# Attention on one core: the turned outputs and maxima leave the scores' banks for the maxima's banks, and VectorE reads them

## What is computed

```python
scores = jnp.einsum('bhqd,bhkd->bhqk', q, k) / jnp.sqrt(jnp.float32(HEAD_DIM))
causal = jnp.tril(jnp.ones((t, t), dtype=bool))          # first layer only
scores = jnp.where(causal[None, None], scores, -jnp.inf)
attn = jax.nn.softmax(scores, axis=-1)
out = jnp.einsum('bhqk,bhkd->bhqd', attn, v)
```

## Time and profile before

| what | us |
| --- | --- |
| median of 3 runs | 5106.11 |
| lowest, highest | 5089.62, 5106.27 |
| the profiled execution | 5106.96 |
| its span, first to last instruction | 5105.2 |
| its mean granted TensorE clock | 0.967 of full |

### The profile page before, as it was taken

The page is one execution under the profiler, slowest core; times in us unless marked ns, Lnnn a source line. Parts: engine busy times, 40 slices in busy tenths (PEclk is TensorE's granted clock), DMA queues, the critical chain, the costliest instruction groups (busy, mean ns, idle before and its releaser), DMA issues. The chain is left out here.

```text
span 5105.2 us, 103667 instructions
## 1 busy us (share of the span) xinstructions
PE 4890.6 (96%) x42852; PEld 2041.1 (40%) x42852; DVE 4444.0 (87%) x5078; ACT 3781.3 (74%) x7207; POOL 375.3 (7%) x546
## 2 busy tenths in 40 slices
PE   8799999999999899779999999999999999999998
PEld 5333333333333466434443333333333333333443
DVE  7799988988876599479999999999999999998346
ACT  3377887887887433338888888888888888888853
POOL 4100000000000233300000000000000000000120
PEclk9699999999999899979999999999999999999999
DMA  6301010010000000430001010000100000000000
GB/s 192 92 11 38 8 41 8 14 41 8 14 8 2 15 14 9 160 88 6 6 11 41 8 34 12 5 8 8 35 11 7 5 8 5 8 4 2 9 1 33
DMA packets 140172, 131.52 MB, mean 26 GB/s; under 512 B 62389, under 2 KB 99573, under 8 KB 139701
## 3 DMA queue, kind: packets, MB, share of 16 engines
q1 hardware_dynamic: 130724, 119.03, 7.8%
q10 hardware_dynamic: 8976, 5.86, 0.7%
HBM read 76.75 MB, written 46.66 MB: 24 GB/s over the span
## 5 line engine op out<-in xcount | busy, mean ns | idle before, releaser
L1529 DVE TENSOR_REDUCE att_mx<-ps 128x2 f32<-128x1024 f32 (+2 forms) x3200 | 3724.3, 1192 | 267.1 <-PE ps L1367 169.8
L1506 ACT ACTIVATE att_probs<-ps 128x512 f32<-128x512 f32 (+3 forms) x6400 | 3378.4, 583 | 623.8 <-PE ps L1430 273.6
L1470 PE MATMUL ps<-att_probs,att_V 128*17 128x256 f32 (+1 forms) x22016 | 1722.1, 387 | 0.3 <-ACT att_outT L1522 0.2
L1430 PE MATMUL ps<-att_Q,K 50*128 50x512 f32 (+3 forms) x5632 | 1457.9, 490 | 23.1 <-ACT att_probs L1506 22.1
L1367 PE MATMUL ps<-K,att_Q 48*128 48x512 f32 (+3 forms) x6400 | 1363.5, 407 | 74.8 <-DVE att_mx L1529 41.5
L1430 PEld LDWEIGHTS ps<-att_Q,K 50*128 50x128 f32 x5632 | 566.8, 184 | 1191.3 <-ACT att_probs L1506 1100.7
L1470 PEld LDWEIGHTS ps<-att_probs,att_V 128*17 128x17 f32 x22016 | 373.6, 96 | 918.6 <-issue 510.6
L1367 PEld LDWEIGHTS ps<-K,att_Q 48*128 48x128 f32 x6400 | 645.3, 190 | 151.9 <-DVE att_mx L1529 107.0
L1461 PE MATMUL ps<-att_probs,att_V 128*17 128x256 f32 x3072 | 238.9, 387 | 0.1
L1425 PE MATMUL ps<-att_Q,K 50*128 50x256 f32 x1536 | 206.5, 330 | 1.3 <-ACT att_probs L1506 1.3
L1866 POOL MEMSET mix_power<- 128x1 f32 x1 | 0.1, 98 | 2642.6 <-POOLq L132 2642.6
(11 more groups left out here) (216 smaller groups left out, 2589.1 us busy)
## 6 DMA issues: line engine op xcount, KB each, us to landing
att_Q<-qhi_scratch SPq DMA_DIRECT2D x232, 64.0 KB, 2.3
K<-khi_scratch SPq DMA_DIRECT2D x212, 64.0 KB, 2.3
v_scratch<-proj_vpad SPq DMA_DIRECT2D x16, 544.0 KB, 4.1
att_Q<-qlo_scratch SPq DMA_DIRECT2D x116, 64.0 KB, 2.3
att_V<-v_scratch SPq DMA_DIRECT2D x53, 136.0 KB, 2.4
K<-klo_scratch SPq DMA_DIRECT2D x106, 64.0 KB, 2.3
att_Q<-att_negT SPq DMA_DIRECT2D x280, 4.0 KB
proj_x<-in_L_attn_x SPq DMA_DIRECT2D x8, 512.0 KB, 6.5
```

Of the source, the lines that this page charges most:

```text
L1430: mm = pe.matmul(ring(at)[:, lo:QB], K[rows, par_of(u), j, kt * P:(kt + 1) * P], Q[rows, slot_of(u), j, lo:QB], start=True, stop=True)
L1470: mm = pe.matmul(ps[VW * h:VW * h + HV, 6, lo:(part + 1) * (QB // 2)], V[:, par_of(v), kt, HV * h:HV * (h + 1)], probs[:, (n_key[v] + kt) ...
L1506: act.activation(probs[:, (n_key[u] + kt) % PBUFS, h if half_wide(u) else column(h), lo:QB], ring(at)[:, lo:QB], ACT.Exp, scale=SCALE).the ...
L1529: dve.tensor_reduce(mx[:, u % 2, :, j, qt, c], ps[:, 2 + 2 * pair:4 + 2 * pair, 0:max_width(u, i) // 2], AX.X, ALU.max).then_inc(max_taken, 1)
```

## The change

The two turned things leave the ring of score banks. `turn_max` and `turn_out` become entries of the queue that the maxima's bank pairs are dealt from: all maxima and turns stand in one list (`queue`), entry n takes pair n % 2, and TensorE waits before entry n until VectorE has finished entry n - 2.

VectorE, not ScalarE, reads the result. For `turn_max` it copies 32 x 128 values into `negT` (new `keep_turned`). For `turn_out` the reciprocal and the product read the bank itself, so ScalarE's copy and the tile `out` are gone. ScalarE loses L1485 and L1515, 70 instructions of each. `outT` and `rden` get a second buffer.

`turn_out` moves. Before, the outputs of unit u - 1 were turned at the end of key tile 3 of unit u. Now those of unit u - 2 are turned after the first half of key tile 2 of unit u, behind that half's maximum. The last two units of each layer keep their outputs' turn where it was or at the end. The transfer of the maxima (`place_max` on SP) now waits for VectorE's copy.

```diff
@@ order(u)
+                if slot == GH * LAG + 1 and u > 1:
+                    out.append(("turn_out", u - 2))
                 if (u, slot) in turned:
                     out.append(("turn_max", turned[u, slot]))
...
-            if kt == LAG + 1 and u > 0:
+            if kt == LAG + 1 and u == UNITS - 1:
                 out.append(("turn_out", u - 1))
@@ attention
-    RING = ("score", "turn_max", "turn_out")
...
-            at_ring += step[0] in RING
+            at_ring += step[0] == "score"
...
+    first_queue = []
+    for n, (w, i) in enumerate(items[0:n_before]):
+        first_queue.append(("max", w, i))
+        if n == len(maxima(0)) + AFTER_GATHER // 2 - 1:
+            first_queue.append(("turn_max", 0))
+    queue = first_queue + [step for u in range(UNITS) for step in plan[u] if step[0] in ("max", "turn_max", "turn_out")]
+    number = {step: n for n, step in enumerate(queue)}
...
+    def pair_of(step):
+        return number[step] % 2
...
-        outT = sb("outT", [P, QB])
-        out = sb("out", [P, QT, GH, VW])
+        outT = sb("outT", [P, 2, QB])
@@ SP
-                def place_max(turned_at, u):
-                    sp.wait_ge(emptied, turned_at + 4)
+                def place_max(u):
+                    sp.wait_ge(max_taken, number["turn_max", u] + 3)
@@ PE
-                def take_max(i, u, at, pair):
+                def take_max(u, i):
                     j, qt, c = maxima(u)[i]
-                    pe.wait_ge(max_taken, at + 1)
+                    pair = pair_of(("max", u, i))
+                    pe.wait_ge(max_taken, number["max", u, i] + 1)
...
-                def turn_max(count, at):
-                    pe.wait_ge(neg_steps, count * NEG_STEPS + NEG_STEPS)
-                    pe.transpose(ring(at)[:, 0:P], negp[:], ident[:]).then_inc(scored, 1)
+                def turn_max(u):
+                    step = ("turn_max", u)
+                    pe.wait_ge(max_taken, number[step] + 1)
+                    pe.wait_ge(neg_steps, u * NEG_STEPS + NEG_STEPS)
+                    pe.transpose(ps[:, 2 + 2 * pair_of(step), 0:P], negp[:], ident[:]).then_inc(max_scored, 1)
+
+                def turn_out(v):
+                    step = ("turn_out", v)
+                    pe.wait_ge(max_taken, number[step] + 1)
+                    pe.wait_ge(out_kept, v + 2)
+                    for t in range(tiles(v)):
+                        mm = pe.transpose(ps[:, 2 + 2 * pair_of(step), t * P:(t + 1) * P], outT[:, v % 2, t * P:(t + 1) * P], ident[:])
+                    mm.then_inc(max_scored, 1)
@@ ACT
-                        elif what == "turn_out":
-                            n = tiles(step[1])
-                            act.activation(out[:, 0:n].rearrange("p t h e -> p (t h e)"), ring(at)[:, 0:n * P], ACT.Copy
-                                           ).then_inc(emptied, 1)
@@ DVE
+                def keep_turned(u):
+                    step = ("turn_max", u)
+                    dve.wait_ge(max_scored, number[step] + 1)
+                    if u >= 2:
+                        dve.wait_ge(max_got[u % 2], 64 * (u // 2))
+                    dve.tensor_copy(negT[:, u % 2, :], ps[0:PARTS * NEG, 2 + 2 * pair_of(step), 0:P]).then_inc(max_taken, 1)
...
                             v = step[1]
-                            dve.wait_ge(emptied, at + 4)
                             n = tiles(v)
-                            dve.reciprocal(rden[:, 0:n], out[:, 0:n, :, HD]).then_inc(out_recip, 1)
+                            out = ps[:, 2 + 2 * pair_of(step), 0:n * P].rearrange("p (t h e) -> p t h e", t=n, h=GH)
+                            dve.wait_ge(max_scored, number[step] + 1)
+                            dve.reciprocal(rden[:, v % 2, 0:n], out[:, :, :, HD]).then_inc(out_recip, 1)
```

More of the change, by code:

```diff
@@ L1218, in attention, with last_max @@
         n_key.append(n_key[-1] + keys(u))
-    turned_at = {step[1]: at for u in range(UNITS) for step, at in zip(plan[u], place[u]) if step[0] == "turn_max"}
-    turned_at[0] = -1
+    first_queue = []
[5 more added lines that the diff above has]
+    number = {step: n for n, step in enumerate(queue)}
+    assert len(number) == len(queue)
+    def pair_of(step):
+        return number[step] % 2
+    def last_max(u):
+        return "max", u, len(maxima(u)) - 1
     NEG = GH * QT
@@ L1245, in attention @@
         negT = sb("negT", [PARTS * NEG, 2, P], F32R)
-        rden = sb("rden", [P, QT, GH])
+        rden = sb("rden", [P, 2, QT, GH])
         if causal:
@@ L1334, in _ @@
                     load_queries(w)
-                place_max(-1, 0)
+                place_max(0)
                 for u in range(UNITS):
@@ L1402, in _ @@
                     first_keys(w, i)
-                    take_max(i, w, n, n % 2)
+                    take_max(w, i)
                     if not causal and n >= n_before - 14:
@@ L1414, in _ @@
                         what = step[0]
-                        if what in RING:
+                        if what == "score":
                             pe.wait_ge(emptied, at + 1)
@@ L1476, in _ @@
                         elif what == "turn_out":
-                            pe.wait_ge(out_kept, step[1] + 2)
-                            for t in range(tiles(step[1])):
-                                mm = pe.transpose(ring(at)[:, t * P:(t + 1) * P], outT[:, t * P:(t + 1) * P], ident[:])
-                            mm.then_inc(scored, 1)
+                            turn_out(step[1])
             @block.scalar
             def _(act):
-                def keep_turned(par, at):
-                    act.activation(negT[:, par, :], ring(at)[0:PARTS * NEG, 0:P], ACT.Copy).then_inc(emptied, 1)
                 for piece in range(FIRST if causal else NQB):
                     fetch_keys(act, 0, piece, k_first[piece], v_first[piece])
-                act.sem_inc(emptied, 2)
+                act.sem_inc(emptied, 3)
                 act.sem_inc(out_kept, 1)
-                act.wait_ge(scored, 1)
-                keep_turned(0, -1)
                 for u in range(UNITS):
@@ L1519, in _, with reduce_max @@
                             act.wait_ge(values_done, n_key[v + 1] + PBUFS)
+                            if v >= 2:
+                                act.wait_ge(max_scored, number["turn_out", v - 2] + 1)
                             n = tiles(v) * P
-                            act.activation(outT[:, 0:n], ps[:, 6, 0:n], ACT.Copy).then_inc(out_kept, 1)
+                            act.activation(outT[:, v % 2, 0:n], ps[:, 6, 0:n], ACT.Copy).then_inc(out_kept, 1)
             @block.vector
             def _(dve):
-                def reduce_max(i, u, at, pair):
+                def reduce_max(u, i):
                     j, qt, c = maxima(u)[i]
-                    dve.wait_ge(max_scored, at + 1)
+                    pair = pair_of(("max", u, i))
+                    dve.wait_ge(max_scored, number["max", u, i] + 1)
                     dve.tensor_reduce(mx[:, u % 2, :, j, qt, c],
@@ L1548, in _ @@
                 dve.sem_inc(max_taken, 2)
-                dve.sem_inc(out_read, 1)
                 for n, (w, i) in enumerate(items[0:n_before]):
-                    reduce_max(i, w, n, n % 2)
+                    reduce_max(w, i)
                     if n == len(maxima(0)) - 1:
                         gather(0)
+                    if n == len(maxima(0)) + AFTER_GATHER // 2 - 1:
+                        keep_turned(0)
                 for u in range(UNITS):
@@ L1569, in _ @@
                                 o_all[:, first_tile(v):first_tile(v) + n, cols].rearrange("p t (h d) -> p t h d", h=GH),
-                                out[:, 0:n, :, 0:HD], rden[:, 0:n].unsqueeze(3).to_broadcast([P, n, GH, HD]),
-                                ALU.mult).then_inc(out_read, 1)
+                                out[:, :, :, 0:HD], rden[:, v % 2, 0:n].unsqueeze(3).to_broadcast([P, n, GH, HD]),
+                                ALU.mult).then_inc(max_taken, 1)
 LN_STEPS = 4
```

26 lines of the change are left out of this document (10 added, 16 removed).

## The result

| | median, us | lowest to highest | runs | mean granted clock |
| --- | --- | --- | --- | --- |
| before | 5097.86 | 5082.64 to 5106.27 | 4 | 0.967 (profiled one) |
| changed | 5168.27 | 5140.39 to 5179.31 | 4 | 0.961 |

The ratio is 1.0133 [1.0084, 1.0183]: slower, inside the range of 5130 to 5188 and 17 us above the forecast of 5151. The medians differ by 70 us; the forecast was 44 on top of the profiled 5106.96, which lies 9 above the median of before. The profiled execution has a span of 5177.6 us at a clock of 0.958.

The account below looks back on a forecast made before the run. TensorE's queue was taken to set the time, VectorE having about 0.08 us in hand per half. Terms 40 + 1 + 2 + 6 - 4 - 1 = +44 on the profiled 5106.96 gave 5151 us, own range 5138 to 5168, wider range 5130 to 5188.

Parts of the forecast that it names:

- the prediction's 0.49: Layer one, pauses at key tile 2: us lost per us at 1.2 GHz; a fall of 3.4 us costs 1.7.
- B's wait behind the maxima's turn: B, the maximum behind the maxima's turn, waits for the reduction of the maximum before it: 0.75 us on TensorE's path.
- The term of +41: Waits behind the maxima's turns: 52 at 0.77 us for +40, three smaller ones for +1.
- The outputs' turn: +3 predicted (2 + 6 - 4, and -1 for the two ends): Key tile 2: 39 units +2 us, eight double-maximum units +6, eight partly hidden -4; ScalarE's uncovered copies saved -1.
- The copy: VectorE's new copy of the turned maxima: 0.25 us a unit, hidden while TensorE fills the next maximum's banks, cost 0.
- the bound of 17 us: VectorE's copy without cover at all 70 turns: 70 x 0.25 = 17 us.
- The rival: Clock falls at the new waits behind the maxima's turn: a third of 52 places, +29 us, hence 5180; chance 0.20.
- The sign it named: Layer two's granted clock falling below 1.00 would show the clock rival right.
- The reason that the prediction gave against the rival: None of layer two's 37 pauses ended in a clock fall, though five lost 0.8 to 0.9 us.
- The filled pause: Outputs' turn lies wholly in key tile 2's pause, nothing waits at either turn: -30 us, 5077; chance 0.08.
- the vanished lag: VectorE's lag from the gather worked off by the third half, or repaid elsewhere: sum +11, 5118; chance 0.12.

Follow-up runs that it names:

- the second series: The changed kernel run once more, unaltered, beside other runs on one chip: 5143.37 us, ratio 1.0085, clock 0.967.
- The best two: Kernel before with only the outputs' turn changed: 5096.2 us, 0.9992; that kernel with the maximum behind the outputs' turn moved by one half: 5097.98 us, 0.9988.
- the control: Kernel with only the outputs' turn changed, its maxima turned four times in the ring of score banks: 5116.3 us, ratio 1.0032.

## Why the prediction was right, point by point

The profiled runs of the kernels below split into three stretches, one profile for each entry. I took the time at 1.2 GHz out of the first two, at 0.38 us lost for each us at that level. That price is the one by which the two profiles of the changed kernel agree, so their agreement in layer one proves nothing: at the prediction's 0.49 it would read +1 and +12. The wide units stayed at 1.00 and need no price.

| us, against before | layer one | half-wide | 24 wide units | sum |
| --- | --- | --- | --- | --- |
| only maxima's turn | +9 | +5 | +10 | +24 |
| only outputs | -6 | +2 | -5 | -9 |
| changed, two series | +6, +7 | +9, +9 | +15, +18 | +30, +34 |

1. **B's wait behind the maxima's turn: right in place and price.** 0.76 us against 0.75, started by VectorE 0.05 earlier, with the maximum's 0.43 behind it, as the prediction had it.
2. **The term of +41: too large.** The maxima's turn alone measures +28 at equal clock. For some 8 us of the 13 between them the rows show where they went. Wide units come in two lengths. Two rows of the kernel before and the rows above give them:

```profile
3310.45 0.33 PE L1384 MATMUL ps<-ident,att_negp 128*128 128x128 f32 x1
...
3389.72 0.33 PE L1384 MATMUL ps<-ident,att_negp 128*128 128x128 f32 x1
...
3468.98 0.33 PE L1384 MATMUL ps<-ident,att_negp 128*128 128x128 f32 x1
```

   These two units take 79.27 and 79.26; but the one that ends at 3310.45 began at 3230.77 and took 79.68, and 20 of the 24 are of that kind. In the long kind a maximum takes 0.327 to 0.330 us to the values, in the short one 0.318 to 0.320, in most of the 64 halves: 0.4 in all. With only the maxima's turn changed nearly all units are short (80.00). From short to short the turn costs 80.00 - 79.26 = 0.74, as predicted; but 20 units got 0.4 back, some 8 us. The prediction held that a unit can pay nothing back because it has 0.23 us of idle time; the 0.4 came out of time that counts as busy. The other 5 lie in layer one and the half-wide units, and I have not found their cause.
3. **The outputs' turn: +3 predicted (2 + 6 - 4, and -1 for the two ends), measured -7.** In the wide unit it was right. From first to last row of that place B's cost replaces ScalarE's: short unit to short unit, 80.05 against 80.00 for the maxima's turn alone, +0.05 as the sum had it. Of the -7, half lies in layer one (-6 at the price of 0.38, -2 at 0.49), for which the sum had next to nothing, and half in units that are short rather than long (79.38 on the mean against 79.61). What makes them short is open.
4. **The copy: right.** 0.27 us against 0.25, hidden, and a second one is hidden too; the bound of 17 us was not needed.
5. **What the outputs' part and the maxima's part do together: missed.** Alone they give 24 and -9, together 30 to 34. The wide units carry most of it: the two short kinds (79.26 and 80.00) are there, but half or more of the units of the changed kernel are long again (80.38; 80.50 in the second series).
6. **The clock: missed by the forecast, half right as a rival.** The first series ran at 0.961, (0.968 - 0.961) x 4.2 per 0.001 = some 28 us; the second at 0.967, some 5 us. The rival put 17 falls at 1.7 us, 29 us. The first series' median, 5168.27, lies in the rival's band of 5165 to 5200 and just outside the forecast's own 5138 to 5168. The sign it named (layer two's clock below 1.00) is there in both series, in the half-wide units. But in the second series, with the same waits, the whole clock is that of before. The reason that the prediction gave against the rival held for the wide units, which stayed at 1.00. The Trainium skill, "TensorE: Matmul & The Clock Gate", section "A second HAM failure mode: psum-queue depth-cycling", tells of a kernel where small idles while cycling through PSUM banks made the clock swing. This case's rows agree for the half-wide units (0.92 and 0.95, from 1.00), not for the wide ones (1.00), and for layer one in one series of two (0.95 and 0.98, from 0.97).

So the place and the price of the wait were forecast, and the near hit on the time is in part luck, because two errors met: the mechanism was sized at 44 and measures 33 to 38, and the clock, sized at nothing, gave some 28 in the first series and 5 in the second. In the second series, at 5143, the forecast is 8 us too high. The filled pause and the vanished lag, the two ways to a time near or under that of before, did not come: the wait starts from VectorE's recorded end, and the lag was still there in the third half.

No version here beats both kernels. The best two, 0.9992 [0.9971, 1.0013] and 0.9988 [0.9973, 1.0003], cannot be told from the kernel before.

## What to carry to other kernels

Before an entry is added to a two-deep ring of banks, look at the user behind it: it inherits its predecessor's bank, and if the reader of that bank runs at nearly the producer's pace, the producer waits for most of a read, 0.76 us here of a read of 1.23. Moving the user a slot away did not help here: the next one waited instead; a bank that is outside that ring does. Compare kernels at the same granted clock, or one kernel's two series can differ by 25 us, as much as the effect looked for.

## What the runs showed of the hardware

- Time fell by 4.2 us for each 0.001 of mean granted clock, over 45 runs of one kernel from 0.962 to 0.972. Over 5100 us, 0.001 of mean clock is 10.2 us at 1.2 GHz, so a us there costs 4.2 / 10.2 = 0.41 us by this line, and 0.38 by the two profiles of the changed kernel. Why it is less than half a us is not shown.
- Falls to 1.2 GHz came behind waits of under 1 us (0.37 idle before the maximum at 2474.03), and with transposes repeated in both waits the clock was 0.9715 where it was 0.967. With the maxima's repeats alone it was 0.968, and in the control, where nothing waited, 0.9705; so the filling of waits is not shown to be the cause.
- Why the falls gather in the half-wide units while the wide ones, with the same waits, stay at 1.00, is open; so is what sets a unit to one of two lengths 0.4 us apart.
